# Attention units of 512 columns in place of 128 to 512: eleven steps per head group, with the last group's output moved up

## The reference

```python
scores = jnp.einsum('blhd,bmhd->bhlm', q, k) * scale
scores = jnp.where(mask[None, None], scores, -1e30)
attn = jax.nn.softmax(scores, axis=-1)
out = jnp.einsum('bhlm,bmhd->blhd', attn, v)
return out.reshape(B, L, H * DV) @ w_o
```

## Time and profile before

| | |
|---|---|
| Median of 3 runs | 1339.72 us (1336.94 to 1344.49) |
| Profiled execution, own time | 1341.87 us |
| Its span | 1340.0 us |
| Mean granted TensorE clock | 0.961 |
| TensorE, VectorE, ScalarE, GpSimd busy | 1212.5, 822.7, 487.3, 374.5 us |

### The profile page before, as it was taken

How to read it: one execution, slowest core, us unless ns; L and a number is a source line. 1 busy time by engine, 2 the same in 40 slices (tenths; PEclk the granted TensorE clock), 3 DMA queues, 4 the chain that set the end, 5 groups by cost and what they waited for, 6 DMA issues and landing times.

```text
span 1340.0 us, 19647 instructions
## 1 busy us (share of the span) xinstructions
PE 1212.5 (90%) x6073; PEld 760.7 (57%) x6073; DVE 822.7 (61%) x2243; ACT 487.3 (36%) x1124; POOL 374.5 (28%) x462
## 2 busy tenths in 40 slices
PE   6899999999998899988979999998777959999988
PEld 3566566555655466555547777775434436465454
DVE  6477877788688777785433334336684655676431
ACT  2456435552555435552301111111522513525311
POOL 0242023251425423352520000213781450401200
PEclk9799999999999999999989999999888988999989
DMA  9999999999900100010458888872220020000000
GB/s 330 412 420 419 420 421 420 420 419 418 418 23 33 64 1 1 6 58 34 136 139 255 272 268 287 269 246 79 71 68 27 24 71 16 24 7 10 0 16 16
DMA packets 86624, 235.76 MB, mean 176 GB/s; under 512 B 9712, under 2 KB 20624, under 8 KB 86288
## 3 DMA queue, kind: packets, MB, share of 16 engines
q1 hardware_dynamic: 68112, 192.80, 38.8%
q0 software_dynamic: 9216, 25.18, 5.9%
q10 hardware_dynamic: 9216, 16.78, 3.3%
HBM read 66.96 MB, written 167.77 MB: 175 GB/s over the span
## 4 chain that ended last, share of the span: by engine, by line
PE 66%; DVE 21%; issue 5%; ACT 2%; another core or an unknown queue 2%; SPq 2%; DMA 1%; POOL 1%; ACTq 0%; POOLq 0%; DVEq 0%
PE bank L615 6%; PE bank L641 4%; PE bank L1505 4%; PE bank L624 4%; PE bank L1527 4%; PE bank L1766 3%; PE bank L1772 3%; DVE r L1012 3%; DVE negmax L1001 3%; PE bank L712 3%; PE bank L1783 3%; PE bank L542 2%; PE bank L1927 2%; PE bank L1490 2%
## 5 line engine op out<-in xcount | busy, mean ns | idle before, releaser
L829 ACT ACTIVATE r<-bank,negmax 128x128 f32<-128x128 f32 (+3 forms) x256 | 135.2, 528 | 179.7 <-DVE negmax L1001 172.3
L615 PE MATMUL bank<-r 128*128 128x512 f32 (+3 forms) x512 | 185.8, 446 | 2.9 <-ACT r L809 2.9
L1001 DVE TENSOR_REDUCE negmax<-bank 128x1 f32<-128x128 f32 (+3 forms) x256 | 123.9, 485 | 49.5 <-PE bank L616 37.0
L624 PE MATMUL bank<-tables,r 128*128 128x128 f32 x640 | 118.3, 284 | 24.8 <-DVE r L1012 22.5
L1125 POOL TENSOR_TENSOR r<-r,tables 128x256 f32<-128x256 f32 x56 | 40.9, 731 | 338.4 <-ACT r L795 333.0
L1375 POOL DMA_INDIRECT sent<-r,slots x96 | 93.6, 975 | 102.1 <-ACT r L829 52.2
L624 PEld LDWEIGHTS bank<-tables,r 128*128 128x128 f32 x640 | 70.3, 142 | 87.2 <-DVE r L1012 49.7
L1614 DVE COPY r<-bank 128x512 f32<-128x512 f32 x64 | 41.2, 686 | 116.2 <-PE bank L1536 75.0
L1012 DVE TENSOR_SCALAR r<-r,rrow 128x128 f32<-128x128 f32 (+3 forms) x256 | 112.1, 438 | 0.3
L615 PEld LDWEIGHTS bank<-r 128*128 128x128 f32 x512 | 79.2, 194 | 21.4 <-issue 16.8
L1021 DVE COPY late<-bank 128x256 f32<-128x256 f32 (+1 forms) x128 | 60.8, 475 | 29.5 <-PE bank L624 24.4
(11 more groups left out here) (289 smaller groups left out, 2449.4 us busy)
## 6 DMA issues: line engine op xcount, KB each, us to landing
sent<-gath SPq DMA_DIRECT2D x8, 16384.0 KB, 93.7
r<-waT_dram SPq DMA_DIRECT2D x64, 304.0 KB, 3.1
r<-sent SPq DMA_DIRECT2D x64, 256.0 KB, 3.9
sent<-r ACTq DMA_DIRECT2D x64, 256.0 KB
w2buf<-wcT_dram SPq DMA_DIRECT2D x64, 48.0 KB, 3.2
r<-w_o_dram SPq DMA_DIRECT2D x1, 2048.0 KB, 22.5
sent<-gath SPq DMA_DIRECT2D x2, 1024.0 KB, 60.6
out_dram<-x SPq DMA_DIRECT2D x4, 512.0 KB, 2.9
```

Source lines behind the costliest of these rows:

```text
L615: nc.tensor.matmul(at[:, 0:n], QT[g % 2][:, h, i * P:(i + 1) * P], KT[:, 0:n], start=True, stop=False)
L624: last = nc.tensor.transpose(bank[TRANS[u % 2]][:, j * P:(j + 1) * P], prob[:, u % 4, j * P:(j + 1) * P], ident)
L829: nc.scalar.activation(prob[:, u % 4, 0:(i + 1) * P], score_bank(g, u)[:, 0:(i + 1) * P], ACT.Exp, bias=negmax[:, u:u + 1], scale=1.0, acc ...
L1001: nc.vector.tensor_reduce(negmax[:, u:u + 1], score_bank(g, u)[:, 0:(i + 1) * P], axis=AX.X, op=ALU.max, negate=True).then_inc(A["max"], 1)
```

## The change

The list UNITS names the eleven units of a group: tile 0 with all four heads (4 x 128 columns), tile 1 with two heads twice (2 x 256), tiles 2 and 3 with a head each as before. The heads of a unit lie side by side in one score bank and one probability buffer. TensorE makes a score matmul and a mask matmul for each head; VectorE takes all the unit's maxima with one reduction; ScalarE makes one exponential per head; the normalisation of a unit with several heads is a tensor_tensor with the reciprocals broadcast, in place of a tensor_scalar. The slots are 0 to 10, and everything that stood at a slot gets a new one. The latents are made in two halves. In the last group outputs 0 and 1 move to slots 8 and 9; output 2 and the norm of the first half stand before the values of tile 3, and VectorE's residual, statistics, variance and norm of the first half are done within and just behind the last group's slots.

```diff
-        NU = HG * TB
+        UNITS = [(0, range(HG)), (1, range(0, 2)), (1, range(2, HG))]
+        UNITS += [(i, range(h, h + 1)) for i in range(2, TB) for h in range(HG)]
+        NU = len(UNITS)
-        ROPES_AT = {1: 0, 4: 1}
-        LATENTS_AT = 7
-        TURN_AT = {11: 0, 14: 1}
-        PROJECT_AT = {5: 0, 9: 1}
-        VALUES_AT = {12: 0, 16: 1, 20: 2}
+        ROPES_AT = {1: 0, 3: 1}
+        LATENTS_AT = {5: 0, 6: 1}
+        LATENTS_OUT = {7: 0, 8: 1}
+        TURN_AT = {9: 0, 10: 1}
+        PROJECT_AT = {3: 0, 6: 1}
+        OUTPUT_AT = {8: 0, 9: 1}
+        def values_at(g, at):
+            if g % GROUPS == GROUPS - 1:
+                return {6: 0, 10: 1, NU + LAG: 2}.get(at)
+            return {8: 0, 10: 1, NU + 4: 2}.get(at)
...
-            def latent_product(g, at):
+            def latent_product(g, at, part):
+                hg, c = g % GROUPS, slice(part * 2 * P, (part + 1) * 2 * P)
...
             def scores(g, u):
+                for m, h in enumerate(hs):
+                    nc.tensor.matmul(at[:, m * w:(m + 1) * w], QT[g % 2][:, h, i * P:(i + 1) * P], KT[:, 0:w],
+                                     start=(m == 0), stop=False)
+                for m, h in enumerate(hs):
+                    last = nc.tensor.matmul(at[:, m * w + i * P:(m + 1) * w], identb[:], futureb[:],
+                                            start=False, stop=(h == hs[-1]))
...
             def exps(g, u):
+                for m in range(len(hs)):
+                    c, n = slice(m * w, (m + 1) * w), cols.start + m
+                    last = nc.scalar.activation(prob_of(g, u)[:, c], score_bank(g, u)[:, c], ACT.Exp,
+                                                bias=negmax[:, n:n + 1], scale=1.0, accum_out=rowsum[:, n:n + 1])
...
             def normalize(g, u):
+                if len(hs) == 1:
+                    nc.vector.tensor_scalar(p, p, rrow[:, cols], None, ALU.mult).then_inc(A["norm"], 1)
+                else:
+                    p = p.rearrange("p (h n) -> p h n", h=len(hs))
+                    nc.vector.tensor_tensor(p, p, rrow[:, cols].unsqueeze(2).to_broadcast([P, len(hs), w]),
+                                            ALU.mult).then_inc(A["norm"], 1)
```

```diff
-                if b == BATCH - 1 and i < 2:
-                    pe.wait_ge(A["ote"], 3 * GROUPS * (b + 1) - 2)
+                if b == BATCH - 1 and i < TB - 1:
+                    pe.wait_ge(A["ote"], 3 * GROUPS * (b + 1) - (1 if i == TB - 2 else 2))
+                    if i == TB - 2:
+                        pe.wait_ge(A["res"], TB * b + 1)
...
-                slot(b * GROUPS + GROUPS - 1, NU + 4, False)
                 if not more:
                     norm_tensor_half(pe, N1, b, 0, xn1_first, 7)
                     output(b, 2)
+                slot(b * GROUPS + GROUPS - 1, NU + LAG, False)
+                if not more:
                     route_logits(pe, b, 7, HALVES[0], b)
                     output(b, 3)
```

More of the change, by code:

```diff
@@ L548, in rope_product @@
                         .then_inc(A["q"], 1)
-            def latent_product(g, at):
-                hg = g % GROUPS
+            def latent_product(g, at, part):
+                hg, c = g % GROUPS, slice(part * 2 * P, (part + 1) * 2 * P)
                 for p in range(2):
                     h = hg * HG + 2 * p
-                    nc.tensor.matmul(bank[at[p]][:], wl1[:, h:h + 2, :].rearrange("p h c -> p (h c)"), cq1,
+                    nc.tensor.matmul(bank[at[p]][:, c], wl1[:, h:h + 2, :].rearrange("p h c -> p (h c)"), cq1[:, c],
                                      start=True, stop=False)
-                for c in range(0, SEQ, 2 * P):
-                    for p in range(2):
-                        r = slice(QL2 * p, QL2 * (p + 1))
-                        last = nc.tensor.matmul(bank[at[p]][:, c:c + 2 * P], wl2[r, hg, :], cq2[r, c:c + 2 * P],
-                                                start=False, stop=c + 2 * P == SEQ)
-                last.then_inc(A["q"], 1)
+                for p in range(2):
+                    r = slice(QL2 * p, QL2 * (p + 1))
+                    last = nc.tensor.matmul(bank[at[p]][:, c], wl2[r, hg, :], cq2[r, c], start=False, stop=True)
+                if part:
+                    last.then_inc(A["q"], 1)
             def rope_transposes(half, at):
@@ L588, in first_latents @@
                 pe.wait_ge(A["qs"], QSTEPS * g + 2)
-                latent_product(g, (6, 7))
+                for part in range(2):
+                    latent_product(g, (6, 7), part)
             def first_turned(b, half):
@@ L614, in scores @@
                 at = score_bank(g, u)
-                nc.tensor.matmul(at[:, 0:n], QT[g % 2][:, h, i * P:(i + 1) * P], KT[:, 0:n], start=True, stop=False)
-                nc.tensor.matmul(at[:, i * P:n], identb[:], futureb[:], start=False, stop=True)\
-                    .then_inc(A["s"], 1)
+                for m, h in enumerate(hs):
[4 more added lines that the diff above has]
+                                            start=False, stop=(h == hs[-1]))
+                last.then_inc(A["s"], 1)
             def transposes(g, u):
-                i = u // HG
+                i, hs, w, _ = unit(u)
                 pe.wait_ge(A["norm"], NU * g + u + 1)
@@ L651, in slot @@
                     scores(g, at)
-                elif not with_next:
-                    pass
                 if not final and with_next:
@@ L679, in slot @@
                     transposes(g - 1, u + NU)
-                if at in VALUES_AT:
-                    values(g, VALUES_AT[at])
-                elif at + NU in VALUES_AT and not first:
-                    values(g - 1, VALUES_AT[at + NU])
+                if values_at(g, at) is not None:
+                    values(g, values_at(g, at))
+                elif not first and values_at(g - 1, at + NU) is not None:
+                    values(g - 1, values_at(g - 1, at + NU))
                 if g >= GROUPS and not final:
                     route_slot(g // GROUPS - 1, g, at)
-                if g == BATCH * GROUPS - 1 and at in (NU - 2, NU - 1):
-                    output(BATCH - 1, at - NU + 2)
+                if g == BATCH * GROUPS - 1 and at in OUTPUT_AT:
+                    output(BATCH - 1, OUTPUT_AT[at])
             def route_slot(c, g, at):
@@ L825, in exps @@
             def exps(g, u):
-                i = u // HG
+                i, hs, w, cols = unit(u)
                 act.wait_ge(A["max"], NU * g + u + 1)
                 need(act, A["pt"], NU * g + u - 3)
-                nc.scalar.activation(prob[:, u % 4, 0:(i + 1) * P], score_bank(g, u)[:, 0:(i + 1) * P], ACT.Exp,
-                                     bias=negmax[:, u:u + 1], scale=1.0,
-                                     accum_out=rowsum[:, u:u + 1]).then_inc(A["exp"], 1)
+                for m in range(len(hs)):
+                    c, n = slice(m * w, (m + 1) * w), cols.start + m
+                    last = nc.scalar.activation(prob_of(g, u)[:, c], score_bank(g, u)[:, c], ACT.Exp,
+                                                bias=negmax[:, n:n + 1], scale=1.0, accum_out=rowsum[:, n:n + 1])
+                last.then_inc(A["exp"], 1)
             def take_values(g, n):
@@ L1153, in att_pool @@
                     g = GROUPS * b + GROUPS - 1
-                    for u in range(NU):
-                        pool.wait_ge(A["exp"], NU * g + u + 1)
-                        send(b - 1, 2 * TB + u)
+                    for n_sent in range(HG * TB):
+                        pool.wait_ge(A["exp"], NU * g + n_sent * NU // (HG * TB) + 1)
+                        send(b - 1, 2 * TB + n_sent)
         R = {k: sem(f"r_{k}") for k in
```

142 lines of the change are left out of this document (78 added, 64 removed).

## The result

The changed kernel takes 1329.87 us (median of 8 runs, 1324.45 to 1333.79) against 1341.72 for the kernel before (8 runs on the same chip): ratio 0.9923, 95% interval 0.9894 to 0.9952. That is 11.9 us faster, where 26.5 were forecast. The profiled execution took 1332.49 us, its span is 1330.6 against 1340.0, and the mean clock of TensorE is 0.957.

What follows compares the result with a forecast made beforehand. TensorE and VectorE were taken to bound the attention in turn. Gains 6 + 8 + 6 + 4 - 0.2 + 7.5 - 4.8 = 26.5 us, and 2.15 to the median, took 1341.87 to 1313.2; range 1298 to 1336.

Steps and rivals of the forecast that it cites:

- (a): Eleven units for sixteen: less VectorE work in tiles 0 and 1, worth nothing directly; VectorE reaches slot 3 on time.
- (b): Normalisation of tiles 0 and 1 as a tensor_tensor: taken as 0.69 us, bounds 0.48 and 1.06; sum unchanged.
- (e): Latents' matmul cut in two halves: a second mode change costs 0.3 us, bounds 0.1 and 0.4; 4.8 us lost.
- (c), second and third groups: Routing finds room in the new slots: second groups gain 6 us despite a 1.1 us second-values wait, third groups 8.
- (c), first groups: Batches 1 to 3: the norm transposes' wait goes, smaller waits come; 2.0 us net each, 6 us gained.
- (f): GpSimd's sends keep their number and still follow the exponentials in last groups: 0; rope copies keep 2.8 us of cover.
- (c)'s "fourth groups": No ropes cover slots 7 to 9, about 2 us of wait stays; 28 us for 30.3 and 29.8, gain 4.
- (d): Last group to output 3: earlier outputs, values and half's norm remove waits; 48.9 us becomes 41.2 to 41.5, gain 7.5.
- The clock: TensorE's clock, below full in some windows: effect taken as 0, with 1.5 us either way for each of five windows.
- no more room: Rival: routing has no more room, so second, third and fourth groups' 18 us don't come; 1331 us, chance 0.17.
- The waits only move: Rival: waits move, and first groups pay the 0.95 us wait and more; 1337 us, no change, chance 0.09.
- ScalarE takes over: Rival: ScalarE's backlog in slots 7 to 10 holds the next group's scores, 36 us lost; 1349 us, chance 0.08.

Runs made afterwards that it cites:

- runs 1 to 5: Fourth groups' sends issued late (changed kernel 1318.80 us, kernel before 1350.25); changed kernel with weighings earlier 1323.71, latents whole 1320.72, sends gated by value products 1312.22.
- run 4: Changed kernel with the latents made in one piece in slot 6: 1320.72 us, ratio 0.9844 to the kernel before.
- run 5: Changed kernel with the fourth groups' sends gated by the value products in place of the exponentials: 1312.22 us, ratio 0.981 to the kernel before.
- run 7: Changed kernel with the last group's end as in the kernel before: 1320.66 us, ratio 0.9876 to the kernel before.
- run 11 against 9: Changed kernel, sends gated, thirteen of the last group's behind its last values: with the old end 1317.11 us, with the new end 1321.51 us.
- run 6: Changed kernel with the fourth groups' sends left out and GpSimd buffer fills in their place: 1312.43 us (one run).
- run 12: Changed kernel with gated sends in all fourth groups (three, six and seven in the last) and latents in one piece: 1303.13 us, ratio 0.9752.
- run 8: Changed kernel with gated sends, fourth groups' weighings in slots 3, 4 and 6, and latents in one piece: 1313.31 us, ratio 0.9813.
- run 3: Changed kernel with the fourth groups' weighings in slots 3, 4 and 6 in place of 5, 7 and 9: 1323.71 us, ratio 0.9857.

## Why the prediction was half right

The time is in the range (1298 to 1336) and faster, as forecast, but 16.7 us above the forecast: under half of the gain came.

The terms below have the 0.3 us for each of the 16 latents taken off where the latents are made (the last group makes none), from first maximum to first maximum, spans against spans (1340.0 and 1330.6), each rounded by itself; a plus is time gained.

| | forecast | measured | sends left out |
|---|---|---|---|
| before the first group | -0.3 | -1.2 | |
| batch 0 | -1.4 | +1.1 | |
| first groups, three | +5.1 | +8.0 | +8.0 |
| second groups, three | +5.1 | +5.3 | +5.3 |
| third groups, three | +7.1 | +5.5 | +5.5 |
| fourth groups of batches 1 and 2, with the stage behind | +3.4 | -10.3 | +6.2 |
| last group to output 3 | +7.5 | +3.3 | +9.9 |
| what follows | 0 | -2.2 | |
| sum | +26.5 | +9.4 | |

What follows output 3 has the same code in the kernel before, the changed kernel and runs 1 to 5, and took 693.1 to 704.2 us in them, so its -2.2 tells nothing. Nor does the -1.2: the first maximum came at 58.5 to 64.5 us.

**(a): too small. (b): right.** Where TensorE bounds the kernel, (a) had nothing. But with the latents in one piece (run 4) the middle groups of batch 0 take 26.6 us for the 27.0 before, so the rest of the change gives 0.4 us a group there, which pays for the cut in (e); what in it gives them is not shown. The tensor_tensor of 512 probabilities takes 0.69 us at the median and 0.77 in the mean (48 of them), for 0.69 taken; TensorE waits for it 0.5 us in all, in the last group.

```profile
L1047 DVE TENSOR_TENSOR r<-r,rrow 128x512 f32<-128x512 f32 x48 | 36.9, 770 | 0.3
```

**(c), second and third groups: close in size, the wait another one.** Routing found room: 5.3 for 5.1 and 5.5 for 7.1. But the 1.1 us wait of the second values for their evacuation did not come. In batch 3's second group TensorE has one wait, and it is the first value product's, for the ranks (L1306) that VectorE makes in slot 7, where the forecast had none; the second product (550.11) waits for nothing:

```profile
PE bank L668 <- DVE r L1306: 1.6, 1, 1.6
```

```profile
544.98 1.52 PE L668 MATMUL bank<-late,r 128*64 128x256 f32 x12 [1.59 <-DVE r L1306]
```

That the second groups' sum came out is therefore in part luck.

**(c), first groups: direction right, too small for two of three.** 1.5, 3.1 and 3.3 us, 2.0 each less the latents' 0.3 forecast. The wait for the norm's application is gone; the first values wait 0.6 (forecast 0.5), but the second ropes' 0.95 did not come. The waits of TensorE in the first group of batch 1:

```profile
PE bank L668 <- DVE scratch L1269: 0.6, 1, 0.6
PE bank L564 <- ACT r L823: 0.2, 1, 0.2
```

**(f) is the step that failed, and with it (c)'s "fourth groups" and part of (d).** I wrote that the sends "keep their number, those of the last groups follow the exponentials as before: 0". I counted them on GpSimd and asked whether they delay a rope. Their price is on the others: holds of 3.7 and 3.6 us at the second values, and behind each a stretch of 10.2 us at 1.2 GHz. "By slots 28 us for 30.3 and 29.8: gain 2.0 x 2 = 4" was right for the slots: with the sends left out the gain is 3.3 and 2.9. With them it was -5.1 and -5.2, 13.7 us from the forecast's +3.4 in a sum that is 17.1 short. Gating them gave back 7.4 and 7.2 (run 5). The size is this execution's: in run 7, with the same code there, the two windows are 2.0 us longer and 1.2 shorter than in the kernel before.

**(d): under half of its size, and given to the wrong causes.** Forecast 7.5, measured 3.3, and 9.9 without sends. But only 2.8 of that is the moved outputs and norm (run 11 against 9), where my list of waits (2.5, 0.8 of the 2.8, and 0.9) gave them most of it. The 2.5 us wait for the first values' copy was itself the end of a hold of 4.5 us, and the new order did not remove it; it lengthened it to 5.0.

**(e): right in mechanism**, 0.4 for 0.3 a group (run 4), the upper bound. The Trainium skill, "TensorEngine Tiling (Array Packing)", section "Key Properties", has changes of tiling mode drain the array; run 4 agrees in direction, with 0.4 us for each second pass.

**The clock** was put at 0, with 1.5 us either way for each of five windows, because two second groups at 0.96 and 1.00 had taken the same time. That held where VectorE set the pace; behind the fourth groups TensorE sets it, and there 10.2 us at the lower level went with 4.5 us more of busy TensorE than in run 6. The kernel before had 3.4 us at the lower level in batch 1's fourth group (310.8 to 314.2) and none in batch 2's.

The rivals: "no more room" gave 1331, 1 us from what was measured, and is refuted by the second and third groups, which came down by 10.8 us: a rival can hit the time by a mechanism that isn't there. "The waits only move" had 1337 by another wait; "ScalarE takes over" did not come, TensorE waiting 0.2 us for a rope copy. None of them named the sends.

## What to carry to other kernels

Work that is free on its own engine can still have a price at every other one: before moving products about, list what DMA issue runs beside each of them, and look for copies that start late though both sides are done. Place indirect sends behind the products on which the path hangs, in short rows (run 12, 0.9752), and ask what overwrites the rows that they read. A reordering that relies on such gaps must be looked at again after every other edit (run 8), and since the same code had windows of 65.6 and 58.9 us, one profile of each kernel is not enough to price it.

## What was not expected of the hardware

The copy of a finished TensorE product starts 0.05 us after the product's end with no send about and ScalarE free, and up to 5.3 us late (run 3) while indirect sends follow each other at 1.27 us; in the worst case VectorE stood 10.9 us beside a row of fourteen, 9.2 of them with its scores ready. The waiting engines are let go together (307.59 and 307.65). Fills on GpSimd (0.55 us) in the sends' place make no hold. The holds don't follow the core's other transfers: with 419 GB/s in batch 1's window and 33 in batch 2's, they are 3.7 and 3.6 us. Nor does every row make one (run 7). What inside the chip joins the two, and whether the number of sends in flight or the issue of each counts, stays open. Behind a TensorE wait of 2.7 us at such a hold the granted clock went to 1.2 GHz for 10.2 us, with TensorE busy throughout from 308.8 on; in run 3, behind a wait of 3.5 us, it went there for 3.4 in batch 1 and 10.2 in batch 2.
